# A state-space layer with a gated feed-forward: tokens mixed ahead of one product each, and another split of the last normalisation

## The chip, the cores and the metric

The kernel runs on one core of a Trainium2 chip. The metric is device time in microseconds (us). Before the change it is 247.09 us, the median of 3 runs (246.23 to 247.74). Engines: TensorE (PE; PEld its weight loads), VectorE (DVE), ScalarE (ACT), GpSimd (POOL), and SyncE (SP), which issues transfers. All data is fp32.

## The reference, cut to what matters

Two layers stand one behind the other, each with a residual and a normalisation on both sides. The first is a state-space mixer over chunks of 64 tokens; the second is the one that the change touches:

```
x = x + layernorm(mixer(layernorm(x)))                    # x: 8 sequences x 512 tokens x 128
def ffn(x, W_r, W_k, W_v, mu_r, mu_k):
    x_prev = x shifted by one token (zero ahead of the first)
    xr = mu_r * x + (1 - mu_r) * x_prev
    xk = mu_k * x + (1 - mu_k) * x_prev
    r  = sigmoid(xr @ W_r.T)
    return r * (square(relu(xk @ W_k.T)) @ W_v.T)
x = x + layernorm(ffn(layernorm(x)))
```

mu_r and mu_k have one number for each of the 128 channels.

## The kernel before, in words

**Tiles.** The 8 x 512 tokens are 32 tiles of 128 rows: a tile holds 64 tokens of two sequences. Four tiles (q = 0 to 3) make a chunk c of 64 tokens for all sequences; 8 chunks, 32 steps n = 4c + q. After a first part (transposes of x, sums of decays and angles, about 44 us) each engine runs through an order written out by hand, from n = -2 to 31, and then a `last_ffn` of its own. Engines meet by semaphores alone; a waiting instruction holds up all that stands behind it on its engine.

**A step of the mixer.** TensorE (`step`, `mix`): `project_x(n+1)` (L859), `turn(n+1)` (L923, two transposes; it waits for VectorE's mask of step n, `sg_ready`), `project_bc(n+2)` (L851), `y_turn(n-1)` (L1045), `mix(n)` (L946, L952, L958), `score(n+1)` (L937), `y_out(n-1)` (L1054), then `ffn(n)`. VectorE (`step`, L1552): `gated_y(n-1)` (L1397), `state(n-1)` (L1386), `mask(n)` (L1378, tile `sg`), `ffn(n)`, then `weighted_x` in two halves (L1371: `x`, `xg`) with `biased` (L1354) between them, then `rotations(n+2)` (L1359 `rot`, L1364 `turned_bc`). ACT: `x_gate(n+1)` (L660, silu of `project_x`), `turned`, `copy_in`, its part of the feed-forward, `late_yt`, `squares`, `z_gate`, `late_ysq`. POOL: `lower_part` (L425), `ffn`, `early` (L450, L453), `token_factors` (L461, `wx`), `decayed_z` (L468, `zs`), `state` (L476).

**The feed-forward runs behind, by units.** Unit u is chunk u for u = 0 to 6; the last chunk is split into units 7 and 8 of two tiles. In chunk c, at step q:

- q = 0: VectorE `moments(c-2)`; POOL `rstd(c-2)` (a power); TensorE `project_r(c-3)`; ACT `k_relu(c-3)`, `k_square(c-3)`.
- q = 1: VectorE `norm_biases(c-2)` and `last_residual(c-4)` (L1493, four instructions: o = ff * frs + x); ACT `gate_r(c-3)` and `normed(c-2)`; POOL `carry(c-2)` (L504); TensorE `project_v(c-3)`.
- q = 2: VectorE `factor_terms(c-1)`, `gated_v(c-3)`, `stats3(c-3)`; TensorE `turn_normed(c-2)`; ACT `outputs(c-4)` (L757, adds the bias to o).
- q = 3: VectorE `residual(c-1)` (L1444) and `stats2(c-1)`; ACT `turned_x(c-2)`, two copies (L739 into `curT`, L740 into `prevT`, one token later); TensorE `project_k(c-2)`.

The mixing of tokens is in the weights: `mixing_weights` (L1341) makes `w_cur` = mu W and `w_prev` = (1 - mu) W once, and each projection is two products added up in PSUM, one on `curT`, one on `prevT`. `project_k` (L1075) is two products of 128x512; `project_r` (L1093) is eight of 128x128. `carry` (L498) puts the last token of the chunk before into the first column of `prevT`. For units 0 to 4 the transposed tokens `t`, `k`, `r` and `v` share one PSUM bank, number 7, one after the other.

**The tail.** Behind step 31 TensorE's `last_ffn` (L1132) goes: `project_k(5)` (in two parts around `y_turn(31)`), `y_out(31)`, `turn_normed(6)`, `project_r(5)`, `project_k(6)`, `project_v(5)`, `turn_normed(7)`, and so on to `project_v(8)`. VectorE's (L1513) goes: `stats2(6)`, `moments(6)`, `factor_terms(7)`, `gated_y(31)`, `norm_biases(6)`, `residual(7)`, ... ACT's (L760) begins with `late_o(30)`, `normed(6)` in two halves with `late_yt(31)` and `late_ysq(31)` between them, `late_o(31)`, `k_relu(5)`, `turned_x(6)`. The results leave by SP, chunk by chunk, once `outv` has counted them.

Of the kernel before, what the change touches and what calls it, by code (L numbers as in the profile page):

```python
# [25 lines left out]
ALU = mybir.AluOpType  # L26
# [4 lines left out]
L = 64  # L31
# [55 lines left out]
def build(nc, x, w_in, a_log, dt_bias, bc_bias, w_out, w_r, w_k, w_v, mu, consts, out, force_general=False):  # L87
    ctx = ExitStack()
    with ctx:  # L89
# [144 lines left out]
        def flat(buf):  # L234
# [51 lines left out]
        prevT = sb("prevT", 128, 2 * B, L)  # L286
        w_cur = sb("w_cur", 128, 2, D)
# [5 lines left out]
        cnames = ("x1 stats agg mom pow norm_bias normed tr_ps tr_sb carried shifted k_ps k_relu k_act r_ps th "  # L293
                  "v_ps f stats3 res outv").split()
# [37 lines left out]

        def n_of(u):
            return hi(u) - lo(u)
# [70 lines left out]
        def _(pool):  # L405
# [7 lines left out]
            nc.gpsimd.memset(curT[:], 0.0).then_inc(S["st_zero"], 1)  # L413
# [73 lines left out]
            def rstd(k):  # L487
# [5 lines left out]
                wait_past(pool, C["res"], n3)  # L493
# [3 lines left out]
            def carry(c):  # L497

                if c == 0:
                    pool.wait_ge(S["st_zero"], 2)  # L500
                pool.wait_ge(C["tr_sb"], c)
                wait_past(pool, C["r_ps"], c - 1)
                to, of = c % 2 * B, (c + 1) % 2 * B
                nc.gpsimd.tensor_tensor(prevT[:, to:to + B, 0:1], curT[:, of:of + B, L - 1:L],  # L504
                                        one[:].unsqueeze(1).broadcast_to([128, B, 1]), ALU.mult).then_inc(C["carried"], 1)

            def pool_outputs(u, part):
                pool.wait_ge(C["norm_bias"], round3(u) + 1)
# [6 lines left out]
            def ffn(n):  # L515
# [3 lines left out]
                if q == 1 and valid(c - 2):  # L519
                    carry(c - 2)  # L520
                if q == 2 and valid(c - 1):
                    factors(c - 1)

            def last_ffn():
                rstd(6)
                carry(6)
# [3 lines left out]
                carry(7)  # L530
# [33 lines left out]
        def _(act):  # L564
# [126 lines left out]
            def empty_ffn_bank(n):  # L691
# [5 lines left out]
                if q == 3 and valid(c - 2):  # L697
                    turned_x(c - 2)
# [33 lines left out]

            def turned_x(u):
                act.wait_ge(C["tr_ps"], u + 1)
                wait_past(act, C["carried"], chunk_of(u))
                wait_past(act, C["r_ps"], ahead(u) + 1)
                b = sequences(u)
                x_t = ffn_bank("t", u)[:, 0:n_of(u) * 128].rearrange("p (b l) -> p b l", l=L)
                nc.scalar.activation(curT[:, b], x_t, ACT.Copy).then_inc(C["tr_sb"], 1)  # L739
                nc.scalar.activation(prevT[:, b, 1:], x_t[:, :, 0:L - 1], ACT.Copy).then_inc(C["shifted"], 1)  # L740
# [48 lines left out]
            def ffn(n):  # L789
# [5 lines left out]
                if q == 2 and valid(c - 4):  # L795
                    outputs(c - 4)
# [12 lines left out]
        def _(pe):  # L809
# [250 lines left out]
            def turn_normed(u):  # L1060
# [7 lines left out]
                else:  # L1068
                    pe.wait_ge(C["shifted"], 8)
# [4 lines left out]
            def project_k(u, general, part=(0, 1)):  # L1074
                pe.wait_ge(C["tr_sb"], u + 1)  # L1075
                if u == 0:
                    pe.wait_ge(s_mix, 6)
                elif u == 6:
                    pe.wait_ge(S["t_sb"], NT)
                    pe.wait_ge(S["y_ready"], NT)  # L1080
                elif u == 7:
                    pe.wait_ge(C["shifted"], 7)
# [3 lines left out]
                if 0 in part:  # L1086
                    pe.wait_ge(C["shifted"], u + 1)
                    nc.tensor.matmul(k_ps, w_cur[:, 0], cur[:, columns(u)], start=True, stop=False)
                if 1 in part:
                    pe.wait_ge(C["carried"], chunk_of(u) + 1)  # L1090
                    nc.tensor.matmul(k_ps, w_prev[:, 0], prev[:, columns(u)], start=False, stop=True)\
                        .then_inc(C["k_ps"], 1)

            def project_r(u):
                pe.wait_ge(C["tr_sb"], u + 1)
                pe.wait_ge(C["shifted"], u + 1)
# [533 lines left out]
```

## Time and profile before

| | us |
|---|---|
| median of 3 runs | 247.09 (246.23 to 247.74) |
| the profiled execution | 246.15 |
| its span, first to last instruction | 244.3 |
| TensorE busy (matmul) | 215.4, 88% |
| TensorE weight loads | 160.5, 66% |
| VectorE busy | 204.2, 84% |
| ACT busy | 180.0, 74% |
| POOL busy | 140.7, 58% |
| TensorE's granted clock, mean | 0.971 of full |

Busy time is the time in which at least one instruction of an engine runs; instructions of one engine overlap a little, so that the next one's start says more than the last one's end. A page of a profile shows one execution; its span is cut into 40 slices, a digit giving the busy tenths of one (9 is 90% or more). Times in the rows are counted from the start of the span. Several VectorE instructions of one line are merged into one row with their count.

### The profile page before, as it was taken

What the parts mean: (1) busy time and instruction counts of PE and PEld (TensorE: products, weight loads), DVE (VectorE), ACT (ScalarE), POOL (GpSimd) and SP (SyncE); (2) the same over time, 40 slices, a digit from 0 to 9 for tenths busy, and PEclk for the clock granted to TensorE, in tenths of its full rate; (3) what the DMA queues carried; (4) which work ended last, traced back from release to release, by engine and by line L of the source; (5) the groups of instructions that cost most, each with busy time, mean ns of one, the idle gap of its engine ahead of it and who ended that gap; (6) DMA issues with size and microseconds to landing.
All of it is one profiled execution on the core that took longest, in us unless ns stands there. A gap on an engine that the chain in (4) does not pass through costs nothing. (4 is left out here: it accounts for less than half of the span.)

```text
span 244.3 us, 6527 instructions
## 1 busy us (share of the span) xinstructions
PE 215.4 (88%) x1962; PEld 160.5 (66%) x1962; DVE 204.2 (84%) x646; ACT 180.0 (74%) x696; POOL 140.7 (58%) x243
## 2 busy tenths in 40 slices
PE   0896897589899989999999999999999999999930
PEld 0893443347667757668876887788688768757920
DVE  1789999986977998796899899989988996966880
ACT  2366766648887868877987799879879977969661
POOL 7434033745656867757575765867585756544430
PEclk9999799979999999999999999999999999999995
DMA  4980000000000000000000001000100010010123
GB/s 120 226 277 17 0 0 0 1 0 3 1 4 1 3 3 0 4 0 4 0 5 0 3 1 46 4 0 3 43 3 3 13 34 4 1 43 3 43 51 90
DMA packets 10199, 6.45 MB, mean 26 GB/s; under 512 B 864, under 2 KB 9856, under 8 KB 10160
## 3 DMA queue, kind: packets, MB, share of 16 engines
q1 hardware_dynamic: 10016, 5.77, 9.4%
q8 instruction: 18, 0.29, 0.5%
q0 software_dynamic: 144, 0.21, 0.4%
q14 instruction: 21, 0.17, 0.2%
HBM read 3.88 MB, written 2.10 MB: 24 GB/s over the span
## 5 line engine op out<-in xcount | busy, mean ns | idle before, releaser
L958 PE MATMUL bank<-x,sg 64*64 64x256 f32 x256 | 35.5, 397 | 0.0
L660 ACT ACTIVATE bank<-bank,rsn 128x512 f32<-128x512 f32 x32 | 21.1, 659 | 18.3 <-PE bank L859 18.3
L958 PE MATMUL bank<-xg,sg 64*64 64x256 f32 x256 | 33.5, 381 | 0.0
L1371 DVE TENSOR_TENSOR x<-bank,wx 128x512 f32<-128x512 f32 x32 | 21.8, 682 | 13.3 <-ACT bank L660 12.9
L946 PE MATMUL pair<-x,turned_bc 64*64 64x256 f32 x224 | 31.2, 398 | 0.0
L425 POOL TENSOR_TENSOR x_lo<-xnT_all,x_hi 128x128 fp32r<-128x128 f32 x32 | 14.6, 459 | 24.9 <-ACT x_hi L575 24.9
L453 POOL TENSOR_TENSOR rb<-mse,halfn 128x2 f32<-128x2 f32 x32 | 25.1, 786 | 2.5
L1054 PE MATMUL bank<-wo_sb,yt 128*128 128x128 f32 x128 | 22.8, 300 | 0.0
L495 POOL TENSOR_TENSOR frs<-fmo,halfn 128x8 f32<-128x8 f32 (+2 forms) x13 | 15.1, 1160 | 13.2 <-DVE fmo L1463 13.2
L958 PEld LDWEIGHTS bank<-xg,sg 64*64 64x64 f32 x256 | 18.2, 136 | 6.7 <-issue 0.7
L958 PEld LDWEIGHTS bank<-x,sg 64*64 64x64 f32 x256 | 15.4, 135 | 10.1 <-issue 6.1
L649 ACT ACTIVATE junk<-bank 128x64 f32<-128x64 f32 x64 | 13.9, 229 | 10.7 <-DVE bc L1354 8.6
L450 POOL TENSOR_TENSOR mse<-msb,eps_all 128x2 f32<-128x2 f32 x32 | 7.7, 241 | 24.4 <-ACT junk L651 24.4
L1371 DVE TENSOR_TENSOR xg<-bank,wx 128x512 f32<-128x512 f32 x32 | 21.7, 678 | 0.0
L468 POOL TENSOR_TENSOR zs<-zs,ec_all 128x256 f32<-128x256 f32 x32 | 21.4, 669 | 0.0
L952 PE MATMUL bank<-st,bt 64*64 64x256 f32 x128 | 19.8, 387 | 0.5 <-DVE o_all L1306 0.5
L859 PE MATMUL bank<-w_hi,x_hi 128*128 128x512 f32 x32 | 16.9, 527 | 3.7 <-DVE w_lo L1255 2.8
L937 PEld LDWEIGHTS pair<-bt 64*64 64x64 f32 x256 | 17.1, 133 | 4.4
L476 POOL TENSOR_TENSOR st<-sp,f_all 128x256 f32<-128x256 f32 x28 | 18.1, 648 | 1.5 <-DVE sp L1386 1.5
L1054 PEld LDWEIGHTS bank<-wo_sb,yt 128*128 128x128 f32 x128 | 16.7, 190 | 3.2 <-ACT yt L676 0.8
L937 PE MATMUL pair<-bt 64*64 64x64 f32 x256 | 18.1, 219 | 0.0
L1359 DVE TENSOR_TENSOR rot<-bc,cs_all 128x384 f32<-128x384 f32 x32 | 17.5, 548 | 0.0
(193 smaller groups left out, 725.6 us busy)
## 6 DMA issues: line engine op xcount, KB each, us to landing
x_all<-x SPq DMA_DIRECT2D x16, 128.0 KB, 3.8
out<-o_all SPq DMA_DIRECT2D x14, 128.0 KB, 2.4
cm<-consts SPq DMA_DIRECT2D x1, 640.0 KB, 6.6
w_sb<-w_in SPq DMA_DIRECT2D x1, 480.0 KB, 5.8
out<-o_all SPq DMA_DIRECT2D x4, 64.0 KB, 2.1
cm<-consts POOLq DMA_DIRECT2D x1, 128.0 KB, 3.9
wo_sb<-w_out SPq DMA_DIRECT2D x1, 128.0 KB, 4.8
bcb_sb<-bc_bias SPq DMA_DIRECT2D x1, 96.0 KB, 4.2
```

Source lines behind the costliest of these rows:

```text
L453: nc.gpsimd.tensor_tensor(rb[:, par], mse[:], halfn[:, 0:R], ALU.pow).then_inc(S["rb_ready"], 1)
L468: nc.gpsimd.tensor_tensor(zs[:, q].rearrange("p (h e) -> p h e", e=P), zs[:, q].rearrange("p (h e) -> p h e", e=P), at(ec_all, n).unsqueez ...
L476: nc.gpsimd.tensor_tensor(st[:, q].rearrange("p (h e) -> p h e", e=P), sp[:].rearrange("p (h e) -> p h e", e=P), at(f_all, i).unsqueeze(2) ...
L660: nc.scalar.activation(x_ps[:], x_ps[:], ACT.Silu, scale=rsn[:, par:par + 1]).then_inc(S["x_silu"], 1)
L859: mm = nc.tensor.matmul(x_ps[:], a[:, par], b[:, O_X:O_S], start=(k == 0), stop=(k == 2))
L937: mm = nc.tensor.matmul(scores[half(h), r], bt[half(r), par, r, half(h)], bt[half(r), par, 1 - r, half(h)], start=True, stop=True)
L946: mm = nc.tensor.matmul(p_ps[half(1 - h)], turned_bc[half(h), q, 2 * r], rx(x, r)[half(h)], start=(r == 0), stop=(r == R - 1))
L952: mm = nc.tensor.matmul(y_ps[par][half(h)], bt[half(1 - h), par, h, half(h)], state[half(1 - h)], start=True, stop=stop)
L958: mm = nc.tensor.matmul(y_ps[par][half(h)], sg[half(h), a, r], rx(x, r)[half(h)], start=start, stop=stop)
L1054: mm = nc.tensor.matmul(o_ps, yt[:, k], wo_sb[:, k], start=(k == 0), stop=(k == 1))
L1359: vec.tensor_tensor(rot[:], bc[:].rearrange("p (g a n) -> p g a n", g=G3, a=2).unsqueeze(3) .broadcast_to([128, G3, 2, 2, H]), at(cs_all, ...
L1371: vec.tensor_tensor((x1, xg)[a][:, par].rearrange("p (a e) -> p a e", e=P), x_ps[:].rearrange("p (a e) -> p a e", e=P), wx[:, par, a].unsq ...
```

## The change

For units 0 to 5 (`MIX_UNITS = 6`) the tokens themselves are mixed before the products. ACT's `scaled_behind` writes (1 - mu) times the transposed tokens, once for the keys and once for the receptances, one column further on into a new tile `behind` (65 columns a sequence; POOL's `carry_scaled` copies column 64 to column 0 for the next unit). VectorE's `mix` adds mu times the tokens, read from PSUM, and writes the mixed tokens for keys to `curT` and those for receptances to `prevT`. `project_k` is then one product with `wk_sb`, and `project_r` four with `wr_sb`. For unit 5 ACT also writes the last token of each sequence into `prevT`, for unit 6. Units 6 to 8 stay as they were; in the tail `project_k(5)` is no longer split around `y_turn(31)`.

For units 0 to 2 (`POOL_UNITS = 3`) ACT scales and biases the output in one instruction from `ff` (`scaled_f`, in the place of `outputs`, q = 2), and POOL adds x (`add_residual`: two tiles at q = 3 of chunk u+4, two at q = 1 of chunk u+5). VectorE's `last_residual` is left out for them.

```diff
@@ POOL
-            def carry(c):
-                ...
+            def carry_scaled(c):
+                pool.wait_ge(C["mixed"], 2 * c)
+                nc.gpsimd.tensor_tensor(behind[:, :, 0:1], behind[:, :, L:L + 1],
+                                        one[:].unsqueeze(1).broadcast_to([128, 2 * B, 1]), ALU.mult).then_inc(C["carried"], 1)
+            def carry_last():
+                pool.wait_ge(C["tr_sb"], 1)
+                pool.wait_ge(C["r_ps"], 6)
+                ...
+            def add_residual(u, part):
+                for i in range(lo(u), hi(u))[part]:
+                    pool.wait_ge(C["scaled_f"], i + 1)
+                    pool.wait_ge(C["x1"], i + 1)
+                    nc.gpsimd.tensor_tensor(o_all[:, i], o_all[:, i], x_all[:, i], ALU.add).then_inc(C["outv"], 1)
@@ POOL ffn(n)
-                if q == 1 and valid(c - 2):
-                    carry(c - 2)
+                if q == 1 and 1 <= c - 2 < MIX_UNITS:
+                    carry_scaled(c - 2)
...
+                if q == 3 and 0 <= c - 4 < POOL_UNITS:
+                    add_residual(c - 4, slice(0, 2))
+                if q == 1 and 0 <= c - 5 < POOL_UNITS:
+                    add_residual(c - 5, slice(2, 4))
@@ POOL last_ffn
                 rstd(6)
-                carry(6)
                 factors(7)
                 rstd(7)
                 factors(8)
-                carry(7)
+                carry_last()
@@ ACT, q == 3
-                    turned_x(c - 2)
+                    scaled_behind(c - 2)
@@ ACT
+            def scaled_behind(u):
+                act.wait_ge(C["tr_ps"], u + 1)
+                wait_past(act, C["carried"], u)
+                ...
+                for m in range(2):
+                    nc.scalar.activation(behind[:, m * B:m * B + B, 1:], turned_ps(u), ACT.Identity,
+                                         scale=one_less_mu[:, 1 - m:2 - m]).then_inc(C["scaled"], 1)
+                if u == MIX_UNITS - 1:
+                    act.wait_ge(C["r_ps"], u)
+                    nc.scalar.activation(prevT[:, 0:B, 0:1], turned_ps(u)[:, :, L - 1:L], ACT.Copy).then_inc(C["last"], 1)
+            def scaled_f(u):
+                act.wait_ge(C["norm_bias"], round3(u) + 1)
+                act.wait_ge(C["x1"], hi(u))
+                for i in range(lo(u), hi(u)):
+                    k = column3(i)
+                    nc.scalar.activation(o_all[:, i], ff[:, slot(i)], ACT.Identity, scale=frs[:, k:k + 1],
+                                         bias=fnb[:, k:k + 1]).then_inc(C["scaled_f"], 1)
@@ TensorE
+            def tokens_there(u):
+                if u < MIX_UNITS:
+                    pe.wait_ge(C["mixed"], 2 * u + 2)
+                    return
+                ...
@@ TensorE project_k, project_r
+                if u < MIX_UNITS:
+                    nc.tensor.matmul(k_ps, wk_sb[:], cur[:, columns(u)], start=True, stop=True).then_inc(C["k_ps"], 1)
...
+                    if u < MIX_UNITS:
+                        mm = nc.tensor.matmul(r_ps, prev[:, at_i], wr_sb[:], start=True, stop=True)
@@ TensorE last_ffn
-                project_k(5, general, (0,))
+                project_k(5, general)
                 y_turn(NT - 1, 1)
-                project_k(5, general, (1,))
                 y_out(NT - 1)
@@ VectorE
+            def mix(u):
+                dve.wait_ge(C["scaled"], 2 * u + 2)
+                if u == MIX_UNITS - 1:
+                    dve.wait_ge(C["last"], 1)
+                for m, (to, used) in enumerate(((curT, "k_ps"), (prevT, "r_ps"))):
+                    wait_past(dve, C[used], ahead(u) + 1)
+                    vec.scalar_tensor_tensor(out=to[:, sequences(u)], in0=turned_ps(u), scalar=mu_sb[:, 1 - m:2 - m],
+                                             in1=behind[:, m * B:m * B + B, 0:L], op0=ALU.mult,
+                                             op1=ALU.add).then_inc(C["mixed"], 1)
@@ VectorE ffn(n)
-                if q == 1 and valid(c - 4):
+                if q == 1 and valid(c - 4) and c - 4 >= POOL_UNITS:
                     last_residual(c - 4)
@@ VectorE step(n)
                 if within(n + 1):
                     weighted_x(n + 1, (q + 1) % 2, 1)
+                if q == NQ - 1 and valid(n // NQ - 2):
+                    mix(n // NQ - 2)
                 if within(n + 2):
                     rotations(n + 2, (q + 2) % NQ)
```

## Rows read from the trace of the kernel before

**Rows 1.** The page: busy us (share) xinstructions, and TensorE's busy tenths in 40 slices.

```profile
PE 215.4 (88%) x1962; PEld 160.5 (66%) x1962; DVE 204.2 (84%) x646; ACT 180.0 (74%) x696; POOL 140.7 (58%) x243
...
PE   0896897589899989999999999999999999999930
```

**Rows 2.** One chunk by windows: window, length, busy us of each engine, granted clock.

```profile
core 0: us, PE busy (x) PEld busy (x) DVE busy (x) ACT busy (x) POOL busy (x), PEclk, DMA share, GB/s
...
176.40:198.78 22.38, 22.38 (x234) 17.41 (x233) 20.82 (x66) 18.89 (x81) 15.21 (x28) 1.00 0.06 14
```

**Rows 3.** Timeline of TensorE, two steps: start us, us, engine, line, out<-in, shapes, count.

```profile
170.96 0.38 PE L923 MATMUL pair<-cm,turned_bc 128*128 128x128 f32 x2
...
174.68 1.02 PE L1088 MATMUL bank<-curT,w_cur 128*128 128x512 f32 x2
175.54 1.02 PE L1091 MATMUL bank<-prevT,w_prev 128*128 128x512 f32 x2
...
177.09 0.38 PE L923 MATMUL pair<-cm,turned_bc 128*128 128x128 f32 x2
...
180.77 0.39 PE L1111 MATMUL bank<-w_cur,curT 128*128 128x128 f32 x2
...
182.48 0.48 PE L859 MATMUL bank<-w_hi,x_hi 128*128 128x512 f32 x1
```

**Rows 4.** Timeline of VectorE, the same stretch.

```profile
170.36 0.41 DVE L1378 TENSOR_TENSOR sg<-pair,cm 128x256 f32<-128x256 f32 x1
170.69 1.88 DVE L1444 SCALAR_TENSOR_TENSOR x_all<-o_all,tokc,x_all 128x128 f32<-128x128 f32 x4
...
174.13 0.67 DVE L1371 TENSOR_TENSOR xg<-bank,wx 128x512 f32<-128x512 f32 x1
174.73 0.54 DVE L1359 TENSOR_TENSOR rot<-bc,cs_all 128x384 f32<-128x384 f32 x1
...
176.25 0.41 DVE L1378 TENSOR_TENSOR sg<-pair,cm 128x256 f32<-128x256 f32 x1
...
178.05 0.69 DVE L1371 TENSOR_TENSOR x<-bank,wx 128x512 f32<-128x512 f32 x1 [0.63 <-ACT bank L660]
...
181.44 2.04 DVE L1493 SCALAR_TENSOR_TENSOR o_all<-ff,frs,x_all 128x128 f32<-128x128 f32 x4
184.21 0.69 DVE L1371 TENSOR_TENSOR x<-bank,wx 128x512 f32<-128x512 f32 x1 [0.72 <-ACT bank L660]
```

**Rows 5.** Groups of VectorE by line: busy us, mean ns; idle before.

```profile
L1306 DVE SCALAR_TENSOR_TENSOR o_all<-o_all,bank 128x512 f32<-128x512 f32 x1 | 0.7, 689 | 0.0
...
L1346 DVE TENSOR_SCALAR w_cur<-wk_sb,mu_sb 128x128 f32<-128x128 f32 x1 | 0.3, 279 | 0.0
...
L1347 DVE TENSOR_SCALAR wv_half<-wv_sb 128x128 f32<-128x128 f32 x1 | 0.2, 218 | 0.0
```

**Rows 6.** Timelines of POOL, and of VectorE late in the kernel.

```profile
170.77 0.75 POOL L468 TENSOR_TENSOR zs<-zs,ec_all 128x256 f32<-128x256 f32 x1
...
176.66 0.63 POOL L468 TENSOR_TENSOR zs<-zs,ec_all 128x256 f32<-128x256 f32 x1
...
213.22 1.13 DVE L1444 SCALAR_TENSOR_TENSOR x_all<-o_all,tokc,x_all 128x128 f32<-128x128 f32 x4
```

**Rows 7.** Timelines of VectorE, ACT and TensorE around step 31 and behind it.

```profile
214.93 0.86 DVE L1450 BATCH_NORM_STATS2 fst<-x_all 128x6 f32<-128x128 f32 x4
217.46 0.42 DVE L1397 TENSOR_TENSOR y<-bank,zs 128x256 f32<-128x256 f32 x1 [0.29 <-PE bank L958]
...
215.38 0.58 ACT L740 ACTIVATE prevT<-bank 128x504 f32<-128x504 f32 x1
222.36 0.60 ACT L740 ACTIVATE prevT<-pair 128x504 f32<-128x504 f32 x1
...
223.43 1.02 PE L1088 MATMUL bank<-curT,w_cur 128*128 128x512 f32 x2
```

**Rows 8.** Windows early in the kernel, columns as in rows 2.

```profile
45.90:49.30 3.40, 1.53 (x7) 1.09 (x8) 3.32 (x7) 2.61 (x11) 2.51 (x4) 1.00 0.00 0
49.30:52.70 3.40, 3.40 (x33) 1.76 (x33) 2.64 (x6) 1.72 (x10) 1.81 (x4) 0.50 0.00 0
52.70:56.10 3.40, 2.33 (x23) 1.54 (x17) 3.04 (x6) 1.02 (x3) 1.54 (x3) 0.99 0.00 0
```

More of the change, by code:

```diff
@@ L286, in build @@
         prevT = sb("prevT", 128, 2 * B, L)
+        behind = sb("behind", 128, 2 * B, L + 1)
         w_cur = sb("w_cur", 128, 2, D)
@@ L292, in build @@
         ff = sb("ff", 128, 2 * NQ, D)
-        cnames = ("x1 stats agg mom pow norm_bias normed tr_ps tr_sb carried shifted k_ps k_relu k_act r_ps th "
-                  "v_ps f stats3 res outv").split()
+        cnames = ("x1 stats agg mom pow norm_bias normed tr_ps tr_sb carried shifted scaled mixed last k_ps k_relu k_act r_ps th "
+                  "v_ps f stats3 scaled_f res outv").split()
         C = {n: sem("c_" + n) for n in cnames}
@@ L412, in _ @@
             nc.gpsimd.memset(st[:], 0.0).then_inc(S["st_zero"], 1)
-            nc.gpsimd.memset(curT[:], 0.0).then_inc(S["st_zero"], 1)
+            nc.gpsimd.memset(behind[:], 0.0).then_inc(S["st_zero"], 1)
             pool.wait_ge(s_ones, 2)
@@ L1072, in turn_normed, with project_k @@
                 mm.then_inc(C["tr_ps"], 1)
-            def project_k(u, general, part=(0, 1)):
-                pe.wait_ge(C["tr_sb"], u + 1)
-                if u == 0:
-                    pe.wait_ge(s_mix, 6)
-                elif u == 6:
+            def tokens_there(u):
+                if u < MIX_UNITS:
+                    pe.wait_ge(C["mixed"], 2 * u + 2)
+                    return
+                pe.wait_ge(C["tr_sb"], u - MIX_UNITS + 1)
+                pe.wait_ge(C["shifted"], u - MIX_UNITS + 1)
+                if u == MIX_UNITS:
+                    pe.wait_ge(C["last"], 1)
+                    pe.wait_ge(s_mix, 6)
+                else:
+                    pe.wait_ge(C["carried"], MIX_UNITS)
+            def project_k(u, general):
+                tokens_there(u)
+                if u == 6:
                     pe.wait_ge(S["t_sb"], NT)
@@ L1085, in project_k @@
                 k_ps = ffn_bank("k", u)[:, 0:n_of(u) * 128]
-                if 0 in part:
-                    pe.wait_ge(C["shifted"], u + 1)
+                if u < MIX_UNITS:
+                    nc.tensor.matmul(k_ps, wk_sb[:], cur[:, columns(u)], start=True, stop=True).then_inc(C["k_ps"], 1)
+                else:
                     nc.tensor.matmul(k_ps, w_cur[:, 0], cur[:, columns(u)], start=True, stop=False)
[L1089 to L1092, printed above, removed]
+                    nc.tensor.matmul(k_ps, w_prev[:, 0], prev[:, columns(u)], start=False, stop=True)                        .then_inc(C["k_ps"], 1)
             def project_r(u):
-                pe.wait_ge(C["tr_sb"], u + 1)
-                pe.wait_ge(C["shifted"], u + 1)
-                pe.wait_ge(C["carried"], chunk_of(u) + 1)
+                tokens_there(u)
                 if u < 5:
@@ L1110, in project_r @@
                     r_ps, at_i = ffn_bank("r", u)[:, k * D:k * D + D], slice(slot(i) * 128, slot(i) * 128 + 128)
[L1111 to L1112 removed]
+                    if u < MIX_UNITS:
+                        mm = nc.tensor.matmul(r_ps, prev[:, at_i], wr_sb[:], start=True, stop=True)
+                    else:
+                        nc.tensor.matmul(r_ps, cur[:, at_i], w_cur[:, 1], start=True, stop=False)
+                        mm = nc.tensor.matmul(r_ps, prev[:, at_i], w_prev[:, 1], start=False, stop=True)
                 mm.then_inc(C["r_ps"], 1)
@@ L1477, in gated_v @@
                 dve.wait_ge(C["v_ps"], u + 1)
-                wait_past(dve, C["res"], hi(ahead(u)))
+                wait_added(dve, ahead(u))
                 for k, i in enumerate(range(lo(u), hi(u))):
```

48 lines of the change are left out of this document (27 added, 21 removed).

## The prediction

> **What bounds the kernel now.** I read the page's busy shares and slices first, then one settled chunk by windows, then the timelines of that chunk, TensorE beside VectorE, and last the tail. The page has TensorE busy 215.4 of 244.3 us and full in nearly every slice from 105 us on [rows 1]; in the chunk from 176.40 to 198.78 TensorE shows no gap, VectorE 20.82, ACT 18.89 and POOL 15.21 us of 22.38 [rows 2]. That looks like a TensorE bound with room elsewhere. The timelines say more. VectorE has two waits in a chunk, at 178.05 and 184.21, both for ACT's silu of a projection that TensorE has just made. From 184.21 (161.8 a chunk earlier) it has work without a break through the third step and into the fourth, up to the mask `sg`; at 170.36 + 0.41 = 170.77 it ends, and TensorE's next `turn` (L923), which waits for it, starts at 170.96, 0.19 later [rows 3, 4]. So in the fourth step of each chunk VectorE is already level with TensorE. In the step after it the mask ends at 176.66 and `turn` starts at 177.09: with the same 0.19, only 0.24 us are spare there. The gap that the engine totals promise on VectorE lies behind those points, not ahead of them.
>
> **What TensorE loses.** `project_k`: two products 0.86 us apart (174.68, 175.54), one goes: -0.86. `project_r`: 180.77 to 182.48 for eight, four go: -0.86 [rows 3]. That is 1.72 us for each of six units, 10.3 us in all.
>
> **What VectorE gets.** Two 128x512 scalar_tensor_tensor per unit, one input in PSUM. The nearest row is L1306, 689 ns; its scalar is an immediate one, and here it is read from memory, for which the pair L1346 and L1347 shows 279 - 218 = 61 ns [rows 5]. Instructions of this width follow each other about 0.60 us apart (xg at 174.13, its follower at 174.73 [rows 4]), so I take 0.66 each, 1.32 per unit; bounds 1.2 (no price for the scalar) and 1.5 (both durations whole). It stands behind `xg`, ahead of `rotations`, `gated_y`, `state` and `mask` of the next step.
>
> **The turn of a chunk.** The mixed tokens are ready 1.32 after 174.73, at 176.05 + 0.07; `project_k`, which started at 174.68, now starts at about 176.2. Behind it in TensorE's order are `project_x`, `turn` and `project_bc`. `project_k` takes 0.86 instead of 1.72, so `project_x` starts some 0.6 later, and `turn` could come 0.6 later too; but it waits for the mask, and that is 1.32 later, 177.98 + 0.19 = 178.17 instead of 177.09: +1.08. So of the 0.86 saved in `project_k` nothing is left, and the halved `project_r`, later in this step, gives back 0.86. Net +0.22. From there `project_x` leads by silu to VectorE's 184.21, where VectorE's unbroken stretch starts again: the loop closes with 22.6 instead of 22.38. This happens behind units 0 to 4, five times: **+1.1 us**; bounds -0.5 (1.2 for the mixing, and the weights of the restart loaded ahead) and +2.
>
> **What comes out of VectorE** is the last residual of three chunks, 2.04 us at 181.44 [rows 4]. It lies between the mask of the first step and the wait at 184.21, where VectorE is idle already, so it only makes that wait longer: 0. POOL's twelve additions are like its 128x128 differences; POOL is idle 7 us of a chunk [rows 2], and the two additions at a time stand behind `lower_part`, ahead of `early`, which then waits for ACT: 0. If that slack is gone, `wx` comes late, and `x1` with it. ACT's two copies become two scaled ones, its four biases four with scale: about 0.1 us each, 0.5 a chunk, against 3.5 idle: 0; with that slack gone, `late_yt` and so `y_out` come late, and `y_out` stands ahead of a wait of 1.4 us in `project_k`. `carry_scaled` is one small POOL instruction, as before, and waits for nothing late. No transfer is added; the stores of the first chunks leave later and none of them ends the kernel.
>
> **POOL against VectorE.** The four residuals at 170.69 take 1.88 us while POOL's `zs` (from 170.77) runs beside them, and 1.13 at 213.22 with POOL idle [rows 4, 6]: 0.75 lost for a pair of long POOL instructions, some 0.38 for each. Both sides have their inputs in SBUF. The mixing moves `rot` and `turned_bc` (two SBUF inputs each) from 174.73 and 175.3 to 176.05 and 176.6, and POOL's `zs` starts at 176.66 and its `wx` just before. The new additions at the start of the second step fall beside a `rot` as well, in three chunks. From 0 to 0.38 for each of 5 + 3 places, 0 to 3.0; I take a quarter, **+0.7**, since half of these meetings have an instruction that reads PSUM instead. The Trainium skill (SBUF — State Buffer, Who interferes with whom) says that a VectorE instruction with two SBUF inputs and a GpSimd one that reads SBUF exclude each other, whichever comes second waiting for all of the first; the trace agrees with its 1.88 against 1.13. Taken to the letter at each of the eight places it would make this term the upper bound.
>
> **The tail.** In step 31 ACT's second copy for unit 5 ends at 215.38 + 0.58 = 215.96 [rows 7]; with the small new `last` behind it, 216.2. VectorE would go on to `stats2(6)` at 214.93; now it waits for ACT till 216.25 and mixes for 1.32: +2.6. Behind it are `stats2(6)`, `moments(6)`, `factor_terms(7)` and `gated_y(31)`. POOL's power, VectorE's bias, ACT's normalisation, `turn_normed(6)` and ACT's `turned_x(6)` follow each other without slack; that copy ends at 222.36 + 0.60 = 222.96 and then at 225.6. `project_k(6)` started at 223.43, for `project_r(5)` was in front of it: 225.65, **+2.2** [rows 7]. After it TensorE has work almost without a break till it ends, so this reaches the end. Bounds +1.2 (the wait for ACT half as long) and +2.7.
>
> **TensorE's clock.** In 45.90 to 49.30 TensorE was busy 1.53 of 3.40 us; in 49.30 to 52.70 it is granted 0.50 (1.2 GHz), while 52.70 to 56.10 with 2.33 busy is not followed by a fall [rows 8]. In the new tail `gated_y(31)`, at 217.46 before [rows 7], ends near 220.2, while `project_k(5)` is through at 218.8; by the same shifts TensorE then waits 1.9 us for `y_out(31)` and 0.7 for `turn_normed(6)`. I expect one fall there, and half speed for some 3.4 us costs up to 1.7 us of products; 0.5 of it lies in a wait. **+0.8**, 0 to 1.7. The page TensorE: Matmul & The Clock Gate of the Trainium skill (What's actually happening) has the same two states; on it hangs nothing of this.
>
> **Sum**: 1.1 + 0.7 + 2.2 + 0.8 = +4.8 on the profiled execution's 246.15 us (span 244.3 and 1.9 around it): 250.9. That execution lies 0.94 under the median, 247.09, at the lower end of the three; I say **251**.
>
> **Rivals.** (a) *TensorE is the bound, as its totals say.* Then five units give 1.72 each, 8.6 us, and with the tail as above 246.15 - 8.6 + 3.0 = 240.6. For it: no gap on TensorE in 22.38 us. Against: the 0.19 of [rows 3, 4], and PSUM: `k` goes to the very bank that the mixing reads, so `project_k` can't pass it. It decides if the two mixings take under 0.24 us, or VectorE turns out to have slack ahead of `sg`; a part of it (a chunk 0.6 us shorter) gives 245. 12%. The Trainium skill (Perfetto Trace Analysis, Identifying the Most-Contended Engine) says to look for the engine with the highest occupancy, and to judge TensorE by its weight loads, not by matmul busy time; so read, VectorE's 84% against 66% makes it the engine [rows 1], its work grows by 6 x 1.32 - 3 x 2.04 = 1.8 us, and the time would be 248, in the range of (c).
>
> (b) *The clock falls at the turn of each chunk.* TensorE now waits about 1.4 and 0.3 us within 3 us, near the 1.87 of 3.40 idle that went ahead of the fall [rows 8]. At two to five falls of up to 1.7 us: 254 to 259. Against: the waits are shorter than that in all. 13%.
>
> (c) *The additions cancel.* The loop stays at 22.38, ACT is earlier at the end, and no fall: 246.15 + 1.2 + little, 247 to 248.5. 20%.
>
> (d) The forecast, 249 to 254: 55%; about a tenth of it lies under 249.6.
>
> **Chances.** Within 1% is 244.6 to 249.6, about what a measurement here can tell from none. Faster: (a) alone and a bit of (c), 0.14. Same: most of (c) and the low end of (d), 0.24. Slower: (d) and (b), 0.62. The range leaves out (a) and the upper part of (b): 246.8 to 255.
>
> **What would show it.** In a settled chunk: TensorE idle some 1.4 us ahead of `project_k`, ended by VectorE's mixing; `turn` behind it started 0.15 to 0.2 after the mask; `project_r` 0.86 long; the chunk 22.4 to 22.8 us; VectorE idle over 2 us ahead of the second step's `x`. In the tail: a wait of 1 to 1.3 us of VectorE for ACT ahead of the last mixing, `turn_normed(6)` some 2.6 us later against step 31, and a granted clock of 0.50 behind it. I am wrong if a chunk is shorter than 22.2 us, if `project_k` starts without a wait, or if the tail from step 31 is not over 1 us longer.

## The result, and the profile after

After the change the kernel takes **252.43 us** (251.84 to 253.72, 4 runs) against 246.76 (246.23 to 247.74, 4 runs) before: ratio 1.0232 [1.019, 1.0274] (the brackets are a 95% interval): slower, by about 2%. The forecast was 251.0, 246.8 to 255.0. The profiled execution after took 252.89 us, span 251.0; the one before 246.15, span 244.3.

The page after, busy us of each engine and TensorE's clock by slices:

```profile
PE 211.2 (84%) x1902; PEld 155.6 (62%) x1902; DVE 207.3 (83%) x646; ACT 182.5 (73%) x697; POOL 146.8 (59%) x253
...
PEclk9999689999999999999999999999999999985995
```

TensorE has 4.2 us less work than in [rows 1], and the kernel is longer: it now waits. The second thing to see is the 8 and 5 near the end of the clock. Line numbers from here on are those of each kernel's own program.

TensorE's timeline where a chunk turns, the place of [rows 3] (start us, us, engine, line, out<-in, count, [idle before <-releaser]):

```profile
175.96 0.71 PE L1097 MATMUL bank<-wo_sb,yt 128*128 128x128 f32 x4
177.58 1.13 PE L1140 MATMUL bank<-curT,wk_sb 128*128 128x512 f32 x2 [0.91 <-DVE prevT L1537]
...
179.61 0.41 PE L966 MATMUL pair<-cm,turned_bc 128*128 128x128 f32 x2 [0.20 <-DVE sg L1431]
```

VectorE's timeline there, the place of [rows 4]:

```profile
176.13 0.74 DVE L1537 SCALAR_TENSOR_TENSOR curT<-bank,mu_sb,behind 128x512 f32<-128x512 f32 x1
176.79 0.74 DVE L1537 SCALAR_TENSOR_TENSOR prevT<-bank,mu_sb,behind 128x512 f32<-128x512 f32 x1
177.45 0.54 DVE L1412 TENSOR_TENSOR rot<-bc,cs_all 128x384 f32<-128x384 f32 x1
178.03 0.44 DVE L1417 TENSOR_TENSOR turned_bc<-rot 128x192 f32<-128x192 f32 x1
...
179.05 0.41 DVE L1431 TENSOR_TENSOR sg<-pair,cm 128x256 f32<-128x256 f32 x1
...
185.86 0.69 DVE L1424 TENSOR_TENSOR x<-bank,wx 128x512 f32<-128x512 f32 x1 [1.93 <-ACT bank L685]
```

The two mixings stand 0.66 us apart and push `rot` back by 1.32. `project_k`, with nothing left to do behind `y_out`, waits for them; `turn` starts 0.15 after the end of the mask (179.05 + 0.41). The residual that left VectorE shows only in a longer wait ahead of `x`, 1.93 where [rows 4] had 0.72.

The windows of one whole chunk, columns as in [rows 2]; there the same chunk took 22.38 us and TensorE had no gap:

```profile
179.25:202.29 23.04, 21.46 (x223) 16.11 (x222) 20.74 (x64) 19.40 (x81) 17.21 (x32) 1.00 0.06 14
```

The tail, VectorE, ACT and TensorE, the place of [rows 7]:

```profile
218.67 0.75 DVE L1537 SCALAR_TENSOR_TENSOR curT<-bank,mu_sb,behind 128x512 f32<-128x512 f32 x1 [1.31 <-ACT behind L764]
...
220.00 0.86 DVE L1503 BATCH_NORM_STATS2 fst<-x_all 128x6 f32<-128x128 f32 x4
...
222.27 0.43 DVE L1450 TENSOR_TENSOR y<-bank,zs 128x256 f32<-128x256 f32 x1
...
223.86 0.88 ACT L749 ACTIVATE dt_all<-x_all,fnb,frs 128x128 f32<-128x128 f32 x2 [2.88 <-DVE fnb L1527]
...
220.25 1.02 PE L1140 MATMUL bank<-curT,wk_sb 128*128 128x512 f32 x2
222.75 0.44 PE L1088 MATMUL bank<-cm,y 128*128 128x128 f32 x2 [1.48 <-DVE y L1450]
225.06 1.22 PE L1097 MATMUL bank<-wo_sb,yt 128*128 128x128 f32 x4 [1.87 <-ACT yt L701]
226.22 1.12 PE L1114 MATMUL pair<-cm,dt_all 128*128 128x128 f32 x4
...
228.84 1.91 PE L1142 MATMUL bank<-curT,w_cur 128*128 128x512 f32 x2
230.55 1.39 PE L1143 MATMUL bank<-prevT,w_prev 128*128 128x512 f32 x2
231.78 1.05 PE L1182 MATMUL bank<-wv_half,ka 128*128 128x128 f32 x8
```

And its windows (columns as in [rows 2]; the granted clock is the fraction behind POOL's count):

```profile
221.00:224.45 3.45, 0.71 (x3) 0.20 (x2) 1.85 (x15) 0.59 (x2) 2.30 (x2) 1.00 0.00 0
224.45:227.86 3.41, 2.81 (x12) 2.56 (x13) 2.82 (x15) 3.23 (x11) 1.21 (x2) 0.50 0.00 0
227.86:231.28 3.42, 3.42 (x9) 1.99 (x9) 1.42 (x7) 2.48 (x6) 1.93 (x5) 0.50 0.00 0
231.28:236.00 4.72, 4.72 (x39) 4.36 (x37) 2.46 (x15) 3.24 (x7) 2.09 (x4) 1.00 0.24 56
```

TensorE is busy 0.71 of 3.45 us, and is then granted 0.50 (1.2 GHz) for 6.83 us, through `project_r(5)` and all of `project_k(6)`. The trace of before shows 1.00 in this part, up to its last product.

**Where the time is.** I follow the start of ACT's `x_gate`, one in each step, in both traces. Against before it is 0.17 us late ahead of the first mixing, 0.45, 0.73, 0.97, 1.65 and 2.35 in the second step behind the mixing of units 0 to 4. So the loop costs 2.2 and what stands behind it 4.3 of the 6.7 us between the two profiled executions; the 0.17 ahead of the first mixing is no part of the change, for the clock's early falls lie at other places in the two.

### The profile page after: what moved, and what is told of

Same layout as the page of the kernel before. It is cut to its first block and busy times, and to the rows that moved or that the text cites. A ratio compares the mean times of both kernels' runs of the same rounds, so it can differ in the third digit from the quotient of the medians.

```text
span 251.0 us, 6420 instructions
## 1 busy us (share of the span) xinstructions
PE 211.2 (84%) x1902; PEld 155.6 (62%) x1902; DVE 207.3 (83%) x646; ACT 182.5 (73%) x697; POOL 146.8 (59%) x253
## 5 line engine op out<-in xcount | busy, mean ns | idle before, releaser
L1001 PE MATMUL bank<-x,sg 64*64 64x256 f32 x256 | 34.6, 389 | 0.0
L989 PE MATMUL pair<-x,turned_bc 64*64 64x256 f32 x224 | 30.3, 389 | 0.0
L466 POOL TENSOR_TENSOR rb<-mse,halfn 128x2 f32<-128x2 f32 x32 | 24.5, 766 | 2.5
L966 PE MATMUL pair<-cm,turned_bc 128*128 128x128 f32 x64 | 12.7, 280 | 7.8 <-DVE sg L1431 7.8
```

Of the source, the lines that this page charges most:

```text
L466: nc.gpsimd.tensor_tensor(rb[:, par], mse[:], halfn[:, 0:R], ALU.pow).then_inc(S["rb_ready"], 1)
L989: mm = nc.tensor.matmul(p_ps[half(1 - h)], turned_bc[half(h), q, 2 * r], rx(x, r)[half(h)], start=(r == 0), stop=(r == R - 1))
L1001: mm = nc.tensor.matmul(y_ps[par][half(h)], sg[half(h), a, r], rx(x, r)[half(h)], start=start, stop=stop)
```

## The experiments

A chunk is four stretches from one `x_gate` to the next. I call A the one that ends with the fourth step's gate (the expectations call it the fourth step; ACT's outputs, q = 2 in the program, lie in it), B the next, in which the mixing and `project_k` stand, then C and D. The kernel before was measured again with each group of runs, at 246.30 (e5 to e8) to 246.75 us; ratios are to that median, and a difference of some tenths between kernels of different groups is read from the stretches, not from the medians. For chunk 5, in us, from the profiled executions:

| kernel | A | B | C | D | chunk |
|---|---|---|---|---|---|
| before | 5.04 | 5.80 | 6.16 | 5.38 | 22.38 |
| after | 5.84 | 6.18 | 5.66 | 5.38 | 23.06 |
| e1 mixing alone | 5.05 | 6.54 | 5.66 | 5.38 | 22.63 |
| e2 ACT/POOL half alone | 5.84 | 5.81 | 6.17 | 5.37 | 23.19 |
| e11 e2, additions later | 5.42 | 5.79 | 6.17 | 5.37 | 22.75 |
| e12 e11, outputs split | 4.71 | 6.23 | 6.15 | 5.37 | 22.46 |
| e3 unit 5 by weights | 5.85 | 6.17 | 5.67 | 5.38 | 23.07 |
| e6 e3, late mixing | 5.83 | 4.50 | 7.05 | 5.38 | 22.76 |
| e7 e6, stats later | 5.84 | 4.50 | 6.63 | 5.38 | 22.35 |
| e8 e7, outputs a chunk later | 4.52 | 4.69 | 8.43 | 5.37 | 23.01 |
| e9 e7, no ACT/POOL half | 5.17 | 4.50 | 6.77 | 6.58 | 23.02 |
| e10 e7, outputs split | 4.79 | 5.28 | 6.25 | 5.38 | 21.70 |

**e1, the mixing alone** (on after):

```diff
-POOL_UNITS = 3
+POOL_UNITS = 0
```

> Units 0 to 5 mixed as in the changed kernel, the last normalisation left as it was (VectorE's last residual back in three chunks, no additions by POOL). Theory (the loop through VectorE): the residual falls into a wait of VectorE and costs nothing, while POOL's additions beside rot, turned_bc and the token factors go away, some 0.4 us in each of two chunks: 0.8 to 1 us under the changed kernel, 251.5 us. Rival (taking work off VectorE was worth its 2 us a chunk, TensorE's stalls cost the rest): 3 to 6 us over the changed kernel, about 257. The wait ahead of the second step's x should be near 0 in chunks 4 to 6, down from 1.9 us.

Measured 251.56 (250.97 to 252.84), ratio 1.0194 [1.0161, 1.0226] to 246.75. The loop is 0.27 longer at each of five turns (1.34), the tail 4.2 with its half clock. The mixing makes the slowdown, all but 0.9 us. VectorE has no wait left ahead of the second step's `x` in chunks 4 to 6: the residual, back there, fills the 1.93 us, and C and D are as long as after's.

**e2, the ACT/POOL half alone** (on before): `scaled_f`, `add_residual`, and no `last_residual` for units 0 to 2; no mixing.

> The kernel before with the other half of the change alone: outputs of units 0 to 2 scaled by ACT, x added by POOL, no mixing. Theory: VectorE's residual lay in its wait, so nothing is gained; POOL's additions beside rot and turned_bc in the second step push the mask of the fourth step back by up to 0.4 us in three chunks: 0 to +1 us against before, 247 to 248. Rival (VectorE's total is what counts): 2 us less a chunk, 241 to 244.

Measured 249.15 (248.25 to 251.32), 1.0091 [1.0057, 1.0125]: more than I expected. All of it that the loop shows is in A: +0.37, +0.80 and +0.80 in chunks 4 to 6. Two causes lie there, and e11 and e12 part them. Another 0.37 lies behind step 31 in e2, e11 and e12 alike: TensorE's last product ends 23.48 us behind the last gate where it ended 23.11 behind it in before, since VectorE's first aggregation behind `stats2(6)` waits 0.55 us in the place of 0.20. What makes that wait is open; e3, with the same half, has 0.20.

**e11, POOL's second additions one step later** (on e2):

```diff
-                if q == 1 and 0 <= c - 5 < POOL_UNITS:
+                if q == 2 and 0 <= c - 5 < POOL_UNITS:
                     add_residual(c - 5, slice(2, 4))
```

> The kernel of e2 (before, with the POOL/ACT half alone) with POOL's second pair of additions moved from the second step to the third. e2 measured 249.15 against 246.75 before. Theory A (ACT's longer outputs alone make the fourth step late): 249.1, the fourth step of chunks 4 to 6 still 5.41, 5.84, 5.84. Theory B (POOL's additions in the second step, beside VectorE's turned_bc 0.49 instead of 0.36 and its next two 0.36 and 0.56 instead of 0.15 and 0.48, bring 0.43 us a chunk of it in chunks 5 and 6): 248.3, the fourth step 5.4 in all three. Theory C (all of it is the additions): 246.8 to 247.3.

Measured 248.21 (247.48 to 249.59), 1.0048 [1.0022, 1.0074], and A is 5.41, 5.42, 5.42: theory B. In e2 the two additions make POOL itself late, and VectorE's instructions beside POOL's are longer. POOL, then VectorE, in e2:

```profile
165.12 1.22 POOL L519 TENSOR_TENSOR o_all<-o_all,x_all 128x128 f32<-128x128 f32 x2
...
167.47 0.41 POOL L469 TENSOR_TENSOR wx<-w_all,rb 128x128 f32<-128x128 f32 x1
167.85 0.63 POOL L476 TENSOR_TENSOR zs<-zs,ec_all 128x256 f32<-128x256 f32 x1
...
166.06 0.49 DVE L1390 TENSOR_TENSOR turned_bc<-rot 128x192 f32<-128x192 f32 x1
...
167.55 0.36 DVE L1461 TENSOR_TENSOR tokc<-csq_all,eps_all 128x4 f32<-128x4 f32 x1
167.94 0.56 DVE L1463 SCALAR_TENSOR_TENSOR tokc<-tokc 128x4 f32<-128x4 f32 x1
```

And the same in e11:

```profile
167.05 0.40 POOL L469 TENSOR_TENSOR wx<-w_all,rb 128x128 f32<-128x128 f32 x1
...
166.06 0.36 DVE L1390 TENSOR_TENSOR turned_bc<-rot 128x192 f32<-128x192 f32 x1
...
167.40 0.15 DVE L1461 TENSOR_TENSOR tokc<-csq_all,eps_all 128x4 f32<-128x4 f32 x1
167.59 0.49 DVE L1463 SCALAR_TENSOR_TENSOR tokc<-tokc 128x4 f32<-128x4 f32 x1
```

The three are 0.13, 0.21 and 0.07 us longer in e2, 0.41 of the 0.42 by which A is longer in chunks 5 and 6. All these instructions have their inputs in SBUF. Only the first of the three, `turned_bc`, meets an addition, its last 0.28 us. `rot`, which runs beside the additions before that, keeps its 0.55 us, and it is the second addition that takes 0.80 where one takes 0.46 elsewhere. POOL's `wx` is then 0.42 late, and with `zs` it falls beside the two narrow instructions, at 167.55 and 167.94. The Trainium skill (SBUF — State Buffer, Who interferes with whom) has a VectorE instruction with two SBUF inputs and a GpSimd one that reads SBUF exclude each other, the later waiting for the whole of the earlier. The trace agrees in that `rot`, started 0.06 ahead of the second addition, holds it up and not the other way round; it doesn't agree in size for `turned_bc`, longer by 0.13 where 0.28 of the addition was left.

**e12, ACT's outputs split as well** (on e11):

```diff
-                    (scaled_f if c - 4 < POOL_UNITS else outputs)(c - 4)
+                    if c - 4 < POOL_UNITS:
+                        scaled_f(c - 4, slice(0, 2))
+                    else:
+                        outputs(c - 4)
+                if q == 3 and 0 <= c - 4 < POOL_UNITS:
+                    scaled_f(c - 4, slice(2, 4))
```

> The kernel of e11 (before, with the POOL/ACT half alone and POOL's second additions later) with ACT's scaled outputs cut in two, two tiles in its third part (q = 2), two in its fourth (q = 3). e11 measured 248.21, before 246.66. In e11 the x_gate that ends the stretch of the outputs starts without a wait straight behind ACT's own work, as it does in the kernel before, and that stretch is 0.38 us longer in three chunks (5.42 against 5.04), ACT's 1.64 against 1.26 us. Theory (ACT, not VectorE, sets that stretch, so its longer instructions cost their whole difference, and taking two of them away gives it back; the 2.04 us taken from VectorE are worth nothing, since they lie ahead of a wait): the stretch goes to 4.8 to 5.05, the one behind it stays at 5.8, and the time is 246.2 to 247.0, no faster than before by more than 0.5 us. Rival 1 (the residual taken from VectorE is worth something once ACT is out of the way): below 246. Rival 2 (the rest of the cost is POOL beside VectorE, not ACT's length): 247.8 to 248.4, the stretch still 5.42.

Measured 247.42 (246.61 to 249.36), 1.0038 [1.0009, 1.0066]: neither rival, and the theory half right. A fell to 4.71, shorter than before, and B took 0.43 to 0.57 of it back; I had B unchanged. ACT's timeline of before shows why A moved, the lines that I had not read when I priced ACT at nothing:

```profile
168.35 0.23 ACT L649 ACTIVATE junk<-bank 128x64 f32<-128x64 f32 x1 [0.42 <-DVE bc L1354]
...
169.98 1.26 ACT L757 ACTIVATE o_all<-o_all,fnb 128x128 f32<-128x128 f32 x4
...
171.55 0.66 ACT L660 ACTIVATE bank<-bank,rsn 128x512 f32<-128x512 f32 x1
...
177.35 0.66 ACT L660 ACTIVATE bank<-bank,rsn 128x512 f32<-128x512 f32 x1 [0.96 <-PE bank L859]
```

From 168.35 to the gate at 171.55 ACT waits for nothing. It is the third engine that is level there, and 1.64 in the place of 1.26 us of outputs costs its whole 0.38. TensorE's timeline of e12 shows why B took it back:

```profile
176.08 0.71 PE L1085 MATMUL bank<-wo_sb,yt 128*128 128x128 f32 x4
176.63 1.02 PE L1119 MATMUL bank<-curT,w_cur 128*128 128x512 f32 x2
177.49 1.02 PE L1122 MATMUL bank<-prevT,w_prev 128*128 128x512 f32 x2
177.95 0.79 PE L890 MATMUL bank<-w_hi,x_hi 128*128 128x512 f32 x1
```

It has no gap here: with two products for the keys, TensorE bounds A and B together, 10.94 against 10.84 before. And the 2.04 us taken out of VectorE gained nothing, as forecast. By the traces the loop is 0.46 us longer than before's; the rest of the 0.76 is the 0.37 behind step 31 that e2 has too.

**e3, unit 5 left as it was** (on after; `carry(6)` comes back with it, and `project_k(5)` is in two parts again):

```diff
-MIX_UNITS = 6
+MIX_UNITS = 5
```

> The changed kernel with unit 5 by the weights again (MIX_UNITS = 5), so that the tail is the one of before. Theory: the tail took 4.3 of the 6.7 us (VectorE waiting 1.3 us for ACT and mixing for 1.3 ahead of all of unit 6, then TensorE's fall to half clock): 248.0 to 248.8 us, with VectorE's stats2(6) right behind the mask and no granted clock of 0.5 near 225 us. Rival (the loss is spread over the chunks, or is the extra ACT and POOL work): 251 to 252.

Measured 248.17 (247.72 to 248.65), 1.0063 [1.0039, 1.0087]. Behind step 31 it is 0.1 us shorter than before, with the clock at 1.00: 4.3 us of the change are unit 5.

**e4, unit 5 mixed, but out of the way** (on after): `mix(5)` behind `gated_y(31)` on VectorE, `project_k(5)` behind `y_out(31)` on TensorE.

```diff
-                project_k(5, general)
                 y_turn(NT - 1, 1)
                 y_out(NT - 1)
+                project_k(5, general)
```

> The changed kernel with unit 5's mixing put behind gated_y(31) on VectorE and its project_k behind y_out(31) on TensorE; all else as changed. Theory (it is the place in VectorE's order, not the work, that costs in the tail): about as good as unit 5 by weights, 248 to 249 us, no fall of the clock in the tail. Rival (the mixing's own time and ACT's scaled copies are what costs): at most 1.3 us less than the changed kernel, 250.5 to 251.5.

Measured 250.04 (248.3 to 252.22), 1.011 [1.0073, 1.0147]; over its range, and under the rival's. 2.4 of the 4.3 us are gone. TensorE's timeline there:

```profile
220.60 0.41 PE L1088 MATMUL bank<-cm,y 128*128 128x128 f32 x2 [0.72 <-ACT junk_o L713]
222.34 1.22 PE L1097 MATMUL bank<-wo_sb,yt 128*128 128x128 f32 x4 [1.33 <-ACT yt L701]
223.35 1.91 PE L1140 MATMUL bank<-curT,wk_sb 128*128 128x512 f32 x2
```

`project_k(5)` no longer fills the time for which `y_turn` and `y_out` wait, and a fall of the clock to 0.50, for 3.41 us from 222.23 on, comes behind 2.05 us of waits. What the order gave, the clock took in part.

**e5, a third mixing of 0.66 us** at each of the five turns (on after; its result is written over and used by nobody):

```diff
+                    vec.scalar_tensor_tensor(out=xk[:].rearrange("p (b l) -> p b l", l=L), in0=turned_ps(u),
+                                             scalar=mu_sb[:, 1:2], in1=behind[:, 0:B, 0:L], op0=ALU.mult, op1=ALU.add)
```

> The changed kernel with a third instruction like the mixing's two, for units 0 to 4, ahead of them in VectorE's order; it writes a tile that nobody reads. Theory (loop through VectorE): each adds its 0.66 us to the wait ahead of project_k and to the mask behind it, five times: +3.3 us, 255.7, and the chunk longer by 0.66 each. Rival (TensorE's work sets the chunk and VectorE has room): +0 to +1 us.

Measured 258.75 (256.96 to 260.08), 1.0526 [1.0481, 1.0571]: 6.3 us over after's 252.43, not 3.3. The profiled execution is the fastest of the four; in it a turn is 0.8 to 1.0 longer, and TensorE's timeline shows both waits grown:

```profile
205.10 1.12 PE L1140 MATMUL bank<-curT,wk_sb 128*128 128x512 f32 x2 [1.58 <-DVE prevT L1540]
...
207.44 0.41 PE L966 MATMUL pair<-cm,turned_bc 128*128 128x128 f32 x2 [0.52 <-DVE sg L1431]
```

VectorE's work here costs all of its time and a little more. The other executions had a mean clock of 0.948 to 0.954 where this one had 0.967. That fits falls of the clock in the loop, my rival (b), but I have no trace of one of them.

**e6, the mixing behind the next mask** (on e3; `project_k` moved behind the next step's `y_turn`):

```diff
+                if q == 0 and 0 <= n // NQ - 3 < MIX_UNITS:
+                    mix(n // NQ - 3)
                 ffn(n)
...
-                if q == NQ - 1 and 0 <= n // NQ - 2 < MIX_UNITS:
-                    mix(n // NQ - 2)
```

> Unit 5 by the weights (as e3), and for units 0 to 4 the mixing stands behind the mask of the next step on VectorE, and project_k behind y_turn of that step on TensorE. Theory: TensorE no longer waits for the mixing, turn no longer waits for a mask that the mixing has pushed back; what is left of the loop is VectorE's stretch from the silu wait to the first step's mask, 14.98 us by the rows of before, + 0.19 + 6.13 + 0.96 = 22.26 a chunk against 22.65 to 23.1: 1.5 to 2 us under e3, 246.2 to 246.8 us; where ACT's longer scaled_f shows now that project_k no longer hides it, up to 1 us more. Rival (the two waits are only where the loss shows, and it comes back at the next place): as e3, 248.2 us.

Measured 246.58 (245.89 to 248.92), 1.0024 [0.9993, 1.0055], 1.6 under e3: 0.3 a chunk, five times. B lost 1.67, and C, where the mixing is now, took 1.38 back.

**e7, `stats2` later too** (on e6; from q = 3 to q = 0 of the next chunk, behind the mixing):

```diff
-                    stats2(c - 1)
...
                 if q == 0 and valid(c - 2):
+                    stats2(c - 2)
                     moments(c - 2)
```

> As e6, and stats2 of units 0 to 5 moved from the fourth step to the first step of the next chunk, behind the mixing, out of VectorE's stretch that closes the loop and into the time that the last residual has left. Theory: 0.8 us off the loop in each of the chunks 2 to 7, 4 to 4.8 us under e6, 242 to 243 us; POOL's power comes up to 0.5 us later, which the second step's wait covers. Rival (TensorE and VectorE are level in more places than the one): 1 to 2 us under e6.

Measured 243.68 (243.07 to 244.22), 0.9903 [0.9873, 0.9933], 2.9 under e6: 0.8 in each of three chunks, 0.4 in each of the next three; the last step takes 0.6 back. Less than expected: in the first three B shrank by 0.5 to 0.7 and C by 0.1 to 0.2; in the later ones, where ACT makes A long, B stood at 4.50 in e6 already, and only C shrank, by 0.4.

**e8, ACT's four scaled outputs moved to q = 0 of the next chunk** (on e7; POOL's additions follow them).

> As e7, and ACT's scaled outputs (scaled_f) moved from the third step of chunk u+4 to the first step of chunk u+5, where ACT waits 1.6 us, POOL's additions of units 0 and 1 to the third and fourth step there. Theory: in e2 ACT's longer instructions pushed late_yt and with it y_out of the fourth step back by 0.37 us in three chunks, and the additions beside turned_bc cost 0.4 in two: 1 to 1.9 us under e7. Rival (both are hidden once the loop runs through VectorE): 0 to 0.3 us.

Measured 245.02 (244.91 to 245.5), 0.995 [0.9933, 0.9968]: 1.3 over e7, where I had 1 to 1.9 under it. ACT's timeline of e8 behind the mixing:

```profile
176.85 0.60 ACT L787 ACTIVATE ka<-bank 128x512 f32<-128x512 f32 x1 [1.36 <-PE bank L1150]
...
180.50 1.64 ACT L799 ACTIVATE o_all<-ff,fnb,frs 128x128 f32<-128x128 f32 x4
...
182.45 0.65 ACT L692 ACTIVATE bank<-bank,rsn 128x512 f32<-128x512 f32 x1
```

A gains 1.32, and C loses 1.80, for behind its wait for the late keys ACT has no room left ahead of the next gate either.

**e9, e7 without the ACT/POOL half** (`POOL_UNITS = 0`).

> The kernel of e7 with the POOL/ACT half of the change taken out: the last residual of the first three chunks is VectorE's again, ACT copies unscaled, POOL adds nothing. e7 measured 243.68. Theory (the fourth step of chunks 4 to 6 grew from 5.04 to 5.42, 5.84 and 5.84 us because ACT's scaled outputs are longer, and because POOL's additions run beside VectorE's): that step goes back to about 5.05 in all three, -2.0 us; but VectorE's 2.04 us of residual come back in three second steps, where in e7 it is idle 0.55 there and 0.76 in the next step, so up to 0.73 us each is uncovered, +2.2. Sum 243.7 +- 0.7, with the place of the time changed: fourth step of chunks 4 to 6 shorter, second or third longer. Rival 1 (VectorE is no bound in the second step, the residual is hidden): 241.7. Rival 2 (the fourth step's length has nothing to do with ACT's and POOL's half): 245.9, with the fourth step still at 5.8.

Measured 245.11 (244.57 to 246.77), 0.9937 [0.9915, 0.996], 1.4 over e7 and 0.7 over my range; by the stretches of the two traces, 1.2. A fell to 5.17 as the theory has it, but the residual, back on VectorE, cost 0.93 to 1.20 in D of each of the three chunks, where I had at most 0.73. The same half that costs 2.4 us on the kernel before is worth 1.2 to 1.4 here.

**e10, the outputs split** (on e7; the edits of e11 and e12).

> The kernel of e7 with ACT's four scaled outputs per chunk cut in two: tiles 0 and 1 in the third step, 2 and 3 in the fourth (all four were in the fourth), and POOL's second pair of additions a step later than before, in the third step. e7 measured 243.68. Theory (in the fourth step ACT's 1.64 us of scaled outputs stand ahead of its copy of y, which comes late; with half of them there, 0.8 us of cover comes back, and the additions no longer lie beside the second step's rotations): the fourth step 5.84 goes to about 5.3 in chunks 5 and 6 and stays at 5.2 to 5.4 in chunk 4, the third step grows by 0 to 0.2: 242.5 to 243.2. Rival (ACT is full in the third step as well, as it was in the first step of e8): 243.7 to 244.5.

(In the program all four were at q = 2, and two went on to q = 3: from A to B.) Measured **241.59** (241.05 to 243.54), 0.9782 [0.9748, 0.9817]: 5.1 us faster than before and 10.8 than after, and 0.9 under the range. A fell to 4.79, more than I gave it; B grew to 5.28 and C fell from 6.63 to 6.25. VectorE's timeline shows the order that works:

```profile
174.17 0.41 DVE L1447 TENSOR_TENSOR sg<-pair,cm 128x256 f32<-128x256 f32 x1
174.50 0.74 DVE L1553 SCALAR_TENSOR_TENSOR curT<-bank,mu_sb,behind 128x512 f32<-128x512 f32 x1
175.16 0.74 DVE L1553 SCALAR_TENSOR_TENSOR prevT<-bank,mu_sb,behind 128x512 f32<-128x512 f32 x1
175.82 0.86 DVE L1519 BATCH_NORM_STATS2 fst<-x_all 128x6 f32<-128x128 f32 x4
```

The mask leads, the mixing stands where TensorE has `turn`, `project_bc` and `y_turn` to do, and TensorE's `project_k` starts without a wait:

```profile
174.73 0.41 PE L978 MATMUL pair<-cm,turned_bc 128*128 128x128 f32 x2 [0.53 <-DVE sg L1447]
...
175.95 1.12 PE L1152 MATMUL bank<-curT,wk_sb 128*128 128x512 f32 x2
```

## Why the prediction was right, point by point

| term | forecast | measured | from |
|---|---|---|---|
| five turns of a chunk | +1.1 | +1.3 | e1, loop |
| ACT/POOL half, VectorE beside POOL | +0.7 | +0.85 | after less e1, loop |
| the chain in the tail | +2.2 | +2.25 | worked out below |
| the clock in the tail | +0.8 | +2.0 | by subtraction, the rest of 4.3 |
| ahead of the loop, not of the change | 0 | +0.2 | the traces |

**The loop.** The signs came as named: TensorE idle 0.9 to 1.4 us ahead of `project_k`, `turn` 0.15 behind the mask, VectorE's spacing 0.66, a chunk 22.63 long in e1 (22.6 forecast). Only VectorE's idle time ahead of the second step's `x`, 1.93, is a little under what I had named. Rival (a) falls for this change. Its ground was true all the same: in before TensorE is full, and so e12 gained nothing from a relieved ACT and VectorE. e6 to e10 show that its products are worth something once VectorE's work no longer stands ahead of the mask.

**VectorE's residual, priced at 0:** shown by the longer wait ahead of `x`, and by e12, which is no faster without it.

**ACT's longer instructions, priced at 0:** right in the sum, for the wrong reason. I set 0.5 us a chunk against 3.5 idle, a total over the chunk, though the prediction itself had warned of such totals on VectorE. In before, ACT is full in the very stretch of the outputs, and e11 prices it: 0.38 a chunk for three chunks. In the changed kernel it is free, because `project_k` waits for the mixing anyway: A grows by 0.36 in chunk 4 and B shrinks by 0.36 against e1. The 0.85 of the half are then POOL's additions, 0.42 in each of chunks 5 and 6. The contention term was 0.7, put on eight places; the five beside `rot` show next to nothing (0.54 as before, `turned_bc` 0.44 against 0.36), and two chunks carry it, mostly through POOL's late `wx` and `zs`. That its size came out was luck. Its upper bound, called the case in which one waits for all of the other, was not that either: it is 0.38 at eight places, and `zs` alone takes 0.63.

**The tail.** The wait of VectorE for ACT was 1.31. Counted from the last gate, ACT's `dt_all` and with it `turn_normed(6)` came 2.72 late (226.22 - 213.50 against 221.15 - 211.15). With before's 1.81 from `turn_normed(6)` to the end of ACT's copies, `project_k(6)` would have started 2.25 late. It started 3.06 late, and `project_v(5)` behind it 4.27.

**The step that was mis-sized is the clock.** I gave one fall "for some 3.4 us", at most 1.7 us of products, from [rows 8]. The fall lasted twice as long, 6.83 us, through the very products that are heaviest: `project_r(5)`, halved, took 1.71 us (227.13 to 228.84) where the whole took 1.79 before, and `project_k(6)` 2.94 for 1.72. The rows ahead of it are also emptier than those that I had compared: 0.71 busy of 3.45, against 1.53 of 3.40. This 1.2 is most of the distance between 251.0 and 252.4; the medians lie 5.7 apart, the profiled executions 6.7, since that of before is under all the times of its kernel and that of after 0.5 over its median.

**The other rivals.** (c) needed a turn that costs nothing and no fall, and had neither. (b), the clock falling in the loop, did not come with waits of 0.9 to 1.4 us; e5, with up to 2.0, may have met it. The Trainium skill (Perfetto Trace Analysis, Identifying the Most-Contended Engine) takes the engine with the highest occupancy, and judges TensorE by its share of peak FLOP/s and by its weight loads; by the loads that is VectorE here. The runs differ: 6.1 us less work on VectorE gained nothing in e12, and the same 6.1 us are worth 1.2 to 1.4 between e9 and e7, both net of the work that ACT and POOL take over.

## What to carry to other kernels

Where several engines are level, ask of each one, in the stretch where the edit lands, whether its next hand-over starts with a wait; a total over a chunk hides that ACT was full for 3 of its 22 us. Work for a slack engine belongs behind the hand-over for which another engine waits, not ahead of it: the same mixing behind the mask instead of ahead of it, with the statistics, half of ACT's outputs and POOL's second additions moved too and the tail's unit left as it was, turned +2.3% into -2.2%. And in a tail, leave TensorE products that fill its waits: the fall of its clock cost 2.0 us, reckoned by subtraction, on top of 2.25 for the later chain.

## What the runs showed of the hardware that I had not expected

- A fall of TensorE's granted clock to 0.50 in the tail lasted 6.83 us behind 0.71 busy of 3.45 us (after, and e1 alike), and 3.41 us in e4, with waits of 0.72 and 1.33 us. TensorE was busy 2.81 of 3.41 us in the first half of the long one and stayed at half speed.
- Early in the kernel, where nothing was changed, falls came at other places in other executions: before at 25.4 and 49.3 us, e12 at 26.2 (6.83 long) and 56.9. By step 6 that puts a profiled execution 0.6 us ahead of the one of before to 1.9 behind it, so single stretches, not spans, were compared.
- A POOL addition of 128x128 took 0.46 us, and 0.80 beside VectorE's `rot`, which stayed at 0.55 (e2). Beside POOL's `wx` and `zs` a VectorE instruction of 4 columns took 0.36 for 0.15, no less of a loss than the 0.49 for 0.36 of a wide one beside the end of an addition.
